# Linear attention layer: token sums moved ahead of the transposes, output products behind them, and the residual written into the output bank by ScalarE

## What is computed

```python
QKV = jnp.einsum('bsd,ed->bse', X, W_in) + b_in
Q, K, V = jnp.split(QKV, 3, axis=-1)
Q = rope(Q, rot_dim); K = rope(K, rot_dim)
A = jnp.sum(feature_map(K) * V, axis=-2)      # feature_map: K / its norm by token
Y = A[:, None, :] * Q
Y = jnp.einsum('bsd,ed->bse', Y, W_out) + b_out
return Y + X                                  # X is the normalised x; and x + this
```

## Time and profile before

| | us |
|---|---|
| median of 3 runs | 573.84 (573.68 to 574.78) |
| profiled execution, its own time | 573.93 |
| its span, first to last instruction | 572.1 |
| TensorE busy | 560.8 (98%) |
| VectorE busy | 467.1 (82%) |
| ScalarE busy | 371.0 (65%) |
| GpSimd busy | 220.7 (39%) |
| granted TensorE clock, share of full speed | 0.998 |

### The profile page before, as it was taken

The page is one execution under the profiler, slowest core; times in us unless marked ns, Lnnn a source line. Parts: engine busy times, 40 slices in busy tenths (PEclk is TensorE's granted clock), DMA queues, the critical chain, the costliest instruction groups (busy, mean ns, idle before and its releaser), DMA issues.

```text
span 572.1 us, 12875 instructions
## 1 busy us (share of the span) xinstructions
PE 560.8 (98%) x4135; PEld 529.9 (93%) x4135; DVE 467.1 (82%) x1475; ACT 371.0 (65%) x1037; POOL 220.7 (39%) x324
## 2 busy tenths in 40 slices
PE   8999999999999999999999999999999999999996
PEld 8899999999999999999999999999998888888885
DVE  5888789778877997797789778877887899878876
ACT  5987556656765755676556656766976777754543
POOL 3782224233223432332234233223356789613221
PEclk9999999999999999999999999999999999999999
DMA  8806000000000000000000000000000000001012
GB/s 331 296 1 230 2 1 3 1 1 0 0 0 0 0 0 0 0 0 0 0 0 0 0 0 0 0 0 1 2 1 1 1 2 1 1 1 38 2 36 77
DMA packets 9152, 14.71 MB, mean 26 GB/s; under 512 B 1568, under 2 KB 6688, under 8 KB 9120
## 3 DMA queue, kind: packets, MB, share of 16 engines
q1 hardware_dynamic: 8848, 14.04, 6.9%
q10 hardware_dynamic: 272, 0.26, 0.1%
HBM read 12.20 MB, written 2.10 MB: 25 GB/s over the span
## 4 chain that ended last, share of the span: by engine, by line
PE 85%; DVE 6%; POOL 3%; ACT 3%; issue 1%; DMA 0%; DVEq 0%; POOLq 0%
PE bank L655 68%; PE bank L758 5%; PE bank L740 3%; PE bank L761 2%; PE bank L665 2%; PE bank L742 1%; PE bank L871 1%; PE bank L934 1%; ACT prob L1161 1%; PE bank L947 1%; POOL qkv L473 1%; DVE raw L1808 1%; POOL prob L513 0%; ACT big L1134 0%; DVE xn L1775 0%
## 5 line engine op out<-in xcount | busy, mean ns | idle before, releaser
L526 POOL TENSOR_SCALAR prob<-prob,rowinv 128x256 f32<-128x256 f32 (+1 forms) x127 | 96.2, 770 | 267.2 <-DVE rowinv L1589 267.2
L655 PE MATMUL bank<-xT,big 128*128 128x256 f32 x984 | 129.5, 283 | 0.1
L655 PEld LDWEIGHTS bank<-xT,big 128*128 128x128 f32 x984 | 123.2, 191 | 1.0 <-issue 0.2
L1161 ACT ACTIVATE prob<-prob,negmax 128x128 f32<-128x128 f32 (+1 forms) x256 | 112.8, 445 | 8.4 <-DVE negmax L1573 8.4
L655 PE MATMUL bank<-wp,oT 128*128 128x256 f32 x768 | 102.5, 283 | 0.4 <-DVE oT L1519 0.3
L655 PEld LDWEIGHTS bank<-wp,oT 128*128 128x128 f32 x768 | 96.8, 190 | 1.4 <-DVE oT L1519 0.8
L1123 ACT ACTIVATE qT<-bank 128x512 fp32r<-128x512 f32 x68 | 40.6, 597 | 72.2 <-PE bank L655 71.4
L655 PE MATMUL bank<-pT,v 128*128 128x512 f32 (+1 forms) x384 | 79.8, 343 | 0.6 <-DVE pT L1519 0.5
L655 PEld LDWEIGHTS bank<-pT,v 128*128 128x128 f32 x384 | 63.2, 189 | 9.9 <-issue 1.0
L1519 DVE TENSOR_TENSOR pT<-bank,pT 128x512 fp32r<-128x512 f32 (+1 forms) x128 | 65.1, 551 | 3.0 <-ACT pT L1123 2.9
L1123 ACT ACTIVATE pT<-bank 128x512 fp32r<-128x512 f32 (+1 forms) x128 | 55.2, 483 | 12.1 <-PE bank L758 10.0
(11 more groups left out here) (188 smaller groups left out, 1004.6 us busy)
## 6 DMA issues: line engine op xcount, KB each, us to landing
raw<-in_wq SPq DMA_DIRECT2D x4, 512.0 KB, 6.5
raw<-in_wp SPq DMA_DIRECT2D x4, 512.0 KB, 6.9
x<-in_x SPq DMA_DIRECT2D x7, 256.0 KB, 7.1
out<-x SPq DMA_DIRECT2D x6, 256.0 KB, 2.2
raw<-in_w_gu SPq DMA_DIRECT2D x2, 640.0 KB, 5.0
raw<-in_w_in SPq DMA_DIRECT2D x1, 768.0 KB, 4.5
raw<-in_w_down SPq DMA_DIRECT2D x1, 640.0 KB, 6.6
raw<-in_wk SPq DMA_DIRECT2D x1, 512.0 KB, 3.9
```

The lines of the kernel that those rows point to most:

```text
L526: m = pool.tensor_scalar(prob[:, j % 2, 0, a:b], prob[:, j % 2, 0, a:b], rowinv[:, j % 2, r:r + 1], None, ALU.mult)
L655: m = pe.matmul(out, lhs(a), rhs(b), start=first and i == 0, stop=last and i == len(passes) - 1, skip_group_check=True)
L1161: m = act.activation(prob[:, j % 2, i, a:b], prob[:, j % 2, i, a:b], ACT.Exp, scale=-1.0, bias=negmax[:, 2 * i + r:2 * i + r + 1], accum_o ...
```

## The change

Three things are done, all in the linear attention layer.

1. TensorE's order in iteration n becomes `linear_k(n)`, `linear_sum(n - 1)`, `linear_transpose(n + 1)`, `linear_out(n - 2)`, `linear_q(n)`. VectorE does its `linear_sum(n - 1)` ahead of `linear_x_lo(n + 1)` and adds the output bank last.
2. `linear_residual` on ScalarE no longer rewrites x. It writes the residual into the output bank bY (half a bank each for two token tiles), after the bank's last reader is done, and the output products add to it (`start=False`). It stands at the head of the iteration, for batch n − 2. ScalarE's other steps are reordered too: `k_squares(n)` ahead of `linear_x_hi(n + 1)`, and `linear_y(n - 1)` ahead of `weigh(n)`.
3. `linear_bias` on GpSimd is gone (eight instructions). VectorE's `linear_add` writes bank bY + bias row into x, where it added bank and x.

`ln_moments(NB, 0)`, the first moments of the gated layer, moves from the middle of VectorE's iteration 6 to its end. Before the gated layer's loop ScalarE does `linear_residual(7)` between `linear_y(7)` and `hidden_hi(0, 0)`.

```diff
@@ GpSimd @@
-            def linear_bias(n):
-                wait_apart(pool, s_lres1, n + 1)
-                add_row(n, 1).then_inc(s_lres, 1)
...
-                if n > 0:
-                    linear_bias(n - 1)
@@ TensorE @@
             def linear_out(n):
                 pe.wait_ge(s_ly, 2 * n + 2)
                 if n == 0:
                     pe.wait_ge(s_rawl[1], 48)
-                    pe.wait_ge(s_ya, NB)
-                else:
-                    pe.wait_ge(s_la, n)
+                pe.wait_ge(s_lres, n + 1)
...
-                                      start=t + k == 0, stop=t + k == 2, skip_group_check=True)
+                                      start=False, stop=t + k == 2, skip_group_check=True)
...
             def linear(n):
                 if n > 1:
                     linear_k(n, 0)
                     linear_k(n, 1)
-                    linear_out(n - 2)
-                else:
-                    linear_sum(n - 1)
+                linear_sum(n - 1)
                 linear_transpose(n + 1) if n + 1 < NB else gated_transpose(0)
                 if n > 1:
-                    linear_sum(n - 1)
+                    linear_out(n - 2)
@@ ScalarE @@
             def linear_residual(n):
-                act.wait_ge(s_ln, n + 1)
+                act.wait_ge(s_lrs, n + 2)
+                act.wait_ge(*((s_la, n) if n > 0 else (s_ya, NB)))
                 for t in range(ST):
-                    xs = x[:, bass.ds(ST * n + t, 1), :].rearrange("p o d -> p (o d)")
-                    m = act.activation(xs, xs, ACT.Identity, bias=l_scale[:, 1, ST * n + t:ST * n + t + 1],
-                                       scale=l_scale[:, 0, ST * n + t:ST * n + t + 1])
-                m.then_inc(s_lres1, 1)
+                    at = ST * n + t
+                    m = act.activation(bY[:, t * D:(t + 1) * D], x[:, at:at + 1, :].rearrange("p o d -> p (o d)"), ACT.Identity,
+                                       bias=l_scale[:, 1, at:at + 1], scale=l_scale[:, 0, at:at + 1])
+                m.then_inc(s_lres, 1)
...
             def linear(n):
+                if n > 1:
+                    linear_residual(n - 2)
+                    k_squares(n)
                 linear_x_hi(n + 1, (n + 1) % 2) if n + 1 < NB else gated_x_hi(0)
-                if n > 1:
-                    k_squares(n)
+                linear_y(n - 1)
                 weigh(n)
-                linear_y(n - 1)
                 linear_q(n)
...
                 if n == NB - 1:
+                    linear_residual(n - 1)
                     gated_x_hi(1)
-                if n < NB - 1:
-                    linear_residual(n + 1)
...
             linear_y(NB - 1)
+            linear_residual(NB - 1)
             hidden_hi(0, 0)
@@ VectorE @@
+            def linear_add(n):
+
+                dve.wait_ge(s_lo, n + 1)
+                dve.tensor_tensor(x[:, ST * n:ST * (n + 1), :], bY[:, :].rearrange("p (t d) -> p t d", t=ST),
+                                  biases[:, 1:2, :].to_broadcast([P, ST, D]), ALU.add).then_inc(s_la, 1)
...
-                    if n == NB - 2:
-                        ln_moments(NB, 0)
+                    linear_sum(n - 1)
                     if n < NB - 1:
-                        add_bank(n - 2, bY, s_lo, s_lres, s_la)
                         linear_x_lo(n + 1, (n + 1) % 2)
-                        linear_sum(n - 1)
                     else:
                         gated_x_lo(0)
                         gated_apply(1)
-                        linear_sum(n - 1)
-                        add_bank(n - 2, bY, s_lo, s_lres, s_la)
+                    linear_add(n - 2)
```

More of the change, by code:

```diff
@@ L247, in build @@
         s_ln = sem("linear_xn_ready")
-        s_lres = sem("linear_residual_ready")
-        s_lres1 = sem("linear_residual_half")
+        s_lres = sem("linear_residual_in_psum")
         s_lT = sem("linear_xT_in_psum")
@@ L621, in _ @@
             q_rotate(NB - 1)
-            linear_bias(NB - 1)
             def finish(b, q):
@@ L1235, in batch @@
                             linear_x_hi(1, 1)
-                            linear_residual(0)
                         if j == J - 1:
@@ L1477, in _ @@
             k_squares(1)
-            linear_residual(1)
             for n in range(1, NB):
@@ L1857, in linear @@
                 if n == NB - 2:
+                    ln_moments(NB, 0)
                     gated_moments()
@@ L2035, in _ @@
             q_products(NB - 1)
-            add_bank(NB - 2, bY, s_lo, s_lres, s_la)
+            linear_add(NB - 2)
             dve.wait_ge(s_gn, 2)
@@ L2042, in _ @@
             hidden_lo(0, 0)
-            add_bank(NB - 1, bY, s_lo, s_lres, s_la)
+            linear_add(NB - 1)
             gated(0, True, False)
```

## The result

| | before | after |
|---|---|---|
| median, us | 573.88 (573.49 to 574.87) | 572.69 (572.29 to 572.99) |
| ratio | | 0.9976 (0.9968 to 0.9983) |
| profiled execution, us | 573.93 | 572.94 |
| its span, us | 572.1 | 571.1 |

The change makes the kernel 1.2 us (0.2%) faster. The forecast was 2.7 us: the sign held and the time lies in the wide range, but the size was less than half. In a second set of runs the same pair gave 572.36 against 574.32, a ratio of 0.9971 (0.9959 to 0.9983), which is 2.0 us.

The account below looks back on a forecast made before the run. TensorE, 98% busy, was taken as the bound, with gaps from a loop stretched by GpSimd's bias additions. Of 3.7 us winnable, about 1.0 is lost, so 2.7 won: 571.1 us, 8-in-10 range 570.2 to 573.0.

Parts of the forecast that it names:

- wide range: Whole kernel: the time falls between 570.2 and 573.0 us in 8 of 10 cases.
- rival A: Gated layer's start: residual(7) waits for `linear_add(6)`, the first hidden tile slips, 1.2 us lost, 572.3 us; chance 0.14.
- rival B: Each iteration: the residual is late, output products of five iterations wait 0.4 us each, 2.0 lost, 573.1 us; chance 0.10.
- rival C: VectorE's apply: other GpSimd work slides into its place, it stays at 1.4 to 1.8 us, 573.3 us; chance 0.07.
- ceiling of 3.7 us: `linear_k(2)` to the gated layer: the most a better order can win, 50.0 us against 46.3 at TensorE's pace.
- the loop: Weighing to weighing, without TensorE: bias additions stretch VectorE's apply; without them 7.25 us becomes 6.10, below TensorE's 6.84.
- The residual in iterations 2 and 3: ScalarE's weights work stands ahead of the residual, so output products wait: 0.2 us lost in iteration 2, 0.5 in 3.
- slack of 0.45: Iterations 4 and 7: the residual's chain of 4.6 us ends before TensorE needs it at 5.05, so no wait.
- Iteration 7: Last linear iteration: `weigh(7)`, needed by the tail's token sums, comes slightly late; 0.2 us lost, where 0.9 was.
- fills a hole there: zero: VectorE, end of iteration 6: moving `ln_moments` there was claimed to cost zero.
- rival D: Squares waiting for k_copy ahead of x's high part tighten the same loop, 7.5 us lost, 577.6 us; chance 0.07.
- The gated layer's start: Residual(7) ahead of `hidden_hi(0, 0)` delays the first hidden tile's low part 0.5 us; slack 0.85, so hidden.

Follow-up runs that it names:

- e13: e12 with the gated layer's first pair of moments in iteration 4, its `inv_std(NB)` in 5, and `q_products(7)` ahead of the last token-sum product; 571.14 us, 0.9946.
- e1: The kernel before with GpSimd's eight bias additions left out, all orders as before, result incomplete; 571.66 us, ratio 0.9956.
- e2: The changed kernel with an idle GpSimd addition of the same size where the bias addition stood; 575.26 us, ratio 1.0016 to the kernel before.
- e5: The changed kernel with ScalarE's old order of two steps, x's high part ahead of the squares of k; 572.64 us, ratio 0.9969.
- e12: e5 with each ScalarE residual one iteration earlier, behind the copy of q and ahead of all weights work; 571.59 us, ratio 0.9951.
- e6: The changed kernel with the gated layer's first two pairs of moments on VectorE left out; 571.37 us, ratio 0.9951.
- e10: The kernel before with GpSimd's bias additions of batches 0 to 6 kept but moved later, behind VectorE's apply; result complete; 572.71 us, ratio 0.9977.
- e11: The changed kernel with VectorE's old order in iteration 7 alone, the token-sum product behind `gated_apply(1)`; 575.57 us, ratio 1.0023.
- e3: The changed kernel with TensorE's old order in each iteration (k, output products, transposes, sums, q); 582.32 us, ratio 1.0148.

## Why the prediction was right in sign and wrong in size

- **The range.** The forecast's own bounds were gains of 2.0 to 3.6 us, 570.2 to 571.8, and 572.69 is outside them. It lies in the wide range only because rival A's 572.3 and parts of B and C are in it, and A's mechanism did not happen. That is luck.
- **The ceiling of 3.7 us and the loop: right.** e13 comes within 0.3 us of it: 46.58 us from `linear_k(2)` to `gate_and_up(0, 0)`, where the prediction's sum is 46.3. Iterations 4 to 6 of after run at 6.87, 6.76 and 6.77, forecast 6.8 to 6.9. From weighing to weighing ScalarE takes 6.76 (477.14 to 483.91), TensorE's own distance. e1 and e2 show the cause from both sides, 2.28 and 2.38 us. The apply is at 0.74 in two of the four iterations, and at 1.68 and 1.19 in the two others, where the ternary layer's addition and a piece of weights meet it: rival C's mechanism, almost without its price, since n=6 keeps the pace with 1.19 and e2 loses 0.10 with 1.09 and 0.47 with 2.07. The Trainium skill (page "SBUF — State Buffer", section "SBUF: two separate sides") says that of GpSimd and a VectorE instruction in a two-port mode or with two SBUF inputs the first holds the shared ports for the whole instruction. The rows agree in direction: the apply of 478.17 meets a piece of weights on GpSimd that ends at 478.88, and is 0.45 longer, where a full block of both its instructions until 478.88 would make it 0.71 longer.
- **The residual in iterations 2 and 3: about right, one cause missed.** Forecast 0.2 and 0.5, with 0.1 each for restart; against the pace 0.38 and 0.26. Of the 0.38, 0.25 is not the residual: it is the high part behind the squares, which makes `linear_k(3)` wait for its low part, and e5 gives it back. But e5 loses the same 0.25 at n=3, to the residual of batch 1. So the 0.64 of the two iterations together hang on that residual, which the forecast had right, and e12, which moves it, wins 0.31 of them.
- **Iterations 4 to 6, rival B: right that the slack of 0.45 holds.** No wait for the residual there. The pair takes 1.04 us where I took 1.08. One instruction: median 552 ns into the bank, 589 within SBUF. The Trainium skill (page "ScalarE: Activation LUTs", section "Step-by-step: what each stage is for") says that ScalarE writes faster to PSUM than to SBUF, and these medians agree in direction. The page gives no size: the 0.2 us was my guess, and the saving is 0.04 us by pair.
- **"Iteration 7": the step that failed.** I allowed 0.2 and measured 12.01 against 10.76, 1.25 us. I looked at the token sums, which want `weigh(7)`; the wait was one step earlier, for `gated_apply(1)`, and I had not followed that chain. Two items priced at nothing make it up. There is no hole for the moments ("fills a hole there: zero"): the two pairs are on the path, and leaving them out gives 0.80 (e6). And the squares ahead of the high part, whose cost I put into rival D alone: 0.44 (e5). Together 1.24; e13, which changes both, is 1.19 shorter than after. Not all of it is new: e1, with the old orders, has 0.53 above the pace at n=7, so the new orders added 0.72.
- **"The gated layer's start ... Hidden": wrong by 0.34.** The slack that I computed was the hidden tile's. The output products of batch 7 also wait for the new residual, and come 0.23 later. That is a quarter of rival A's size, by another path: in after `linear_add(6)` ends at 498.2, and the residual starts at 499.18, right behind y.
- **The sum.** Losses of 0.38 + 0.26 − 0.12 (iterations 4 to 6) + 1.25 + 0.34 = 2.1 against 1.0 forecast, from the same 3.7: 1.6 are left, and the table has 1.54. The medians of the two sets of runs, 1.2 and 2.0, lie on either side of it.
- **What the reordering is worth: a question I did not ask.** I credited the loop's opening to the change as one thing. By e1 the whole gain is the additions' going, the rest of the change costs 0.74 us, and e10 has as much as the change by moving one step of one engine.

## What to carry to other kernels

When an order that is the same in all iterations is changed, cost its first and its last iteration by themselves: those with foreign work in them, and the start of the next stage, kept 2.2 of the 3.7 us that could be won here. When a step is put ahead of another on one engine, look who waits for the step that is now second, and whether the engine stood idle while it could have done it. And where a GpSimd step stretches a VectorE step that reads and writes SBUF, first try to put it under one that reads a bank (e10), and look what it then pushes back on GpSimd, before rebuilding the stage.

## What the runs showed of the hardware

In e11 TensorE lost part of its clock behind two gaps close together. The clock was at its upper level, 2.4 GHz, until then; the gaps are 1.09 and 1.50 us, with 0.66 of transposes between. The windows (length, busy times, then the granted clock, third from the end) of e11 and of e3:

```profile
480.00:490.00 10.00, 10.00 (x64) 9.14 (x62) 9.29 (x27) 6.66 (x18) 6.26 (x11) 1.00 0.00 0
490.00:500.00 10.00, 7.41 (x34) 6.06 (x33) 6.11 (x19) 5.81 (x14) 2.65 (x6) 0.83 0.00 1
```

```profile
448.00:506.00 58.00, 47.98 (x301) 43.36 (x300) 42.33 (x114) 39.41 (x93) 30.25 (x57) 1.00 0.00 1
```

The sums and output products behind the gaps take 2.67 and 2.40 us from start to start, at a granted clock of 0.66, where after has 1.74 and 1.54: 1.8 of e11's 3.4 us at n=7 are clock, not waiting. By 500 us the clock is back. It did not happen in every execution: e11's twelve have a mean clock of 0.991 to 1.000, and the time follows it, 574.37 us at 1.000 and 576.9 at 0.991. In e3 a single gap of 1.24 to 2.05 us stands in every iteration, 8 to 9.5 us apart, and the clock stays at 1.00. So the same wait can cost more than its length; that it is the nearness of the two gaps that does it is the likely reading of these two kernels, and no run varied it alone.
